# Odd blocks of the delta loop on the other partition half, inverse products on four 64x64 tiles

## The reference, cut to what matters

```python
def step(carry, ins):
    s, mem = carry
    qt, kt, vt, dt, at, bt = ins
    mem = DECAY * mem + dt
    ...                                   # spike of the membrane
    alpha = jax.nn.sigmoid(at + asp * spike)
    beta = jax.nn.sigmoid(bt[..., None] + jnp.sum(spike * bsp, -1, keepdims=True))
    ...
    s = s * alpha[..., None]
    pred = jnp.einsum('bhk,bhkv->bhv', kt, s)
    s = s + (beta * kt)[..., None] * (vt - pred)[:, :, None, :]
    out = jnp.einsum('bhk,bhkv->bhv', qt, s)
    return ((s, mem), out)
```

## Time and profile before

| | |
|---|---|
| median of three runs | 2595.97 us |
| profiled execution | 2596.74 us, span 2594.9 us |
| granted TensorE clock, mean | 0.862 of full speed |
| PE busy | 2186.4 us (84%), 32607 instructions |
| PEld busy | 1506.7 us (58%) |
| DVE busy | 1612.6 us (62%), 4155 instructions |
| ACT busy | 981.7 us (38%) |
| POOL busy | 781.0 us (30%) |
| L2317, ax | 5120 records, 193.9 us busy |
| L2339, xw | 4096 + 1024 records, 140.0 + 33.0 us busy |
| L2293, products of levels 0 to 5 | 6144 records, 128.7 us busy |
| L2308, the 2I of ax | 160 records, 65.1 us busy |

### The profile page before, as it was taken

How to read it: one execution, slowest core, us unless ns; L and a number is a source line. 1 busy time by engine, 2 the same in 40 slices (tenths; PEclk the granted TensorE clock), 3 DMA queues, 4 the chain that set the end, 5 groups by cost and what they waited for, 6 DMA issues and landing times. The chain is left out here.

```text
span 2594.9 us, 76890 instructions
## 1 busy us (share of the span) xinstructions
PE 2186.4 (84%) x32607; PEld 1506.7 (58%) x32607; DVE 1612.6 (62%) x4155; ACT 981.7 (38%) x1930; POOL 781.0 (30%) x884
## 2 busy tenths in 40 slices
PE   7999988999678658899999999999998968963774
PEld 4666656666556323656666666666666737652553
...
GB/s 168 10 10 2 10 10 6 2 2 2 78 37 68 77 118 18 3 27 3 23 7 23 7 23 7 23 7 2 7 3 7 3 54 48 2 33 15 52 53 125
DMA packets 42516, 75.98 MB, mean 29 GB/s; under 512 B 5988, under 2 KB 27244, under 8 KB 39620
## 3 DMA queue, kind: packets, MB, share of 16 engines
...
...
## 5 line engine op out<-in xcount | busy, mean ns | idle before, releaser
L2786 DVE COPY_PREDICATED delta_neg_a_and_p_t<-delta_level_int,bank 128x256 f32<-128x256 uint8 x384 | 179.5, 537 | 65.6 <-PE bank L2293 65.0
L2317 PEld LDWEIGHTS bank<-delta_inverse,delta_neg_a_and_p_t 64*64 64x64 f32 x5120 | 171.4, 141 | 46.1 <-issue 45.6
L2317 PE MATMUL bank<-delta_inverse,delta_neg_a_and_p_t 64*64 64x64 f32 x5120 | 193.9, 228 | 0.0
L2690 POOL TENSOR_TENSOR delta_scaled_beta_k<-delta_scaled_beta_k,delta_decays 128x256 f32<-128x256 f32 x160 | 124.2, 776 | 223.4 <-issue 165.2
L2520 ACT ACTIVATE delta_two_less_ax<-bank 128x512 f32<-128x512 f32 x160 | 94.9, 597 | 243.0 <-PE bank L2317 241.6
L310 PE MATMUL bank<-attn_w_value_out,attn_z_self_t 128*64 128x512 f32 x512 | 144.7, 680 | 40.4 <-DVE attn_cross_attended_t L722 36.3
L699 POOL TENSOR_TENSOR attn_probs<-attn_probs,attn_row_sum 128x512 f32<-128x512 f32 x64 | 65.4, 1042 | 359.4 <-DVE attn_row_sum L781 359.4
L2293 PE MATMUL bank<-weights_sb,delta_scaled_beta_k 64*64 64x64 f32 x6144 | 128.7, 229 | 46.5 <-DVE delta_neg_a_and_p_t L2786 40.8
L2293 PEld LDWEIGHTS bank<-weights_sb,delta_scaled_beta_k 64*64 64x64 f32 x6144 | 110.2, 141 | 82.8 <-DVE delta_neg_a_and_p_t L2786 48.7
L601 ACT ACTIVATE attn_probs_t<-bank 128x512 f32<-128x512 f32 x128 | 71.3, 595 | 197.8 <-PE bank L409 197.8
L2339 PE MATMUL bank<-delta_two_less_ax,delta_inverse_t 64*64 64x64 f32 x4096 | 140.0, 224 | 5.2 <-issue 5.2
...
...
## 6 DMA issues: line engine op xcount, KB each, us to landing
...
```

Of the source, the lines that this page charges most:

```text
L2317: last = pe.matmul(out_[rows(sg), u], AP[rows(sg), hp, eo, b4, 0, :], X[rows(sg), hp, u], start=False, stop=True, skip_group_check=True)
L2690: pool.tensor_tensor(r_[:, :, 0, :], r_[:, :, 0, :], a_[:, :, 1, 0:1].to_broadcast([128, T // (2 * c), c]), ALU.mult)
L2786: last = dve.copy_predicated(second(AP[:, hp, eo, :, :, :].rearrange("p b i n -> p (b i) n"), c), m_, PAIR[hp % 2][eo][:, :].rearrange("p ...
```

## The change

Nothing is computed differently; where things lie and on which part of the array they are multiplied changes, and so does the order.

- AP, X, XT and W have the parity of the block (eo) as their outermost dimension, and a head pair's even or odd units are 256 columns. For even blocks nothing moves. For odd blocks W, XT and the values now lie on the half r = par, where before they lay on sg; X and AP stay on sg. So in ax, xw and y the row half and the column half of odd blocks differ, and those of even blocks are equal.
- Work goes by pairs of head pairs, P = 0 or 1, two head pairs at a time. A product, an ax or an xw is 32 matmuls into two full banks (one for even, one for odd units), where it was 16 matmuls into two half-used banks (products) or one bank (inverse). The inverse has banks 4, 5 for P = 0 and 2, 3 for P = 1; the products of stages 3 to 6 of both P use banks 0 and 1.
- The 2I of ax is written by four bf16 matmuls of 64x64 by 512 columns for each P, where it was one of 128x128 by 512 for each head pair.
- DVE's masked copies take 512 columns where they took 256, half as many. An addition of first_inverse and a transpose of 128x512 becomes three instructions for each P: one of 128x512 for the even units, two of 64x512 for the odd ones, which write to the half that they don't read. Per group that is 30 transposes for 20 and 6 additions for 4. ACT's copies keep their size and number, except those of o (4 of 512 columns for 8 of 256).
- On PE ax(P=0) and ax(P=1) come first, then products and xw of P = 0, a filler, xw and products of P = 1. Norms are summed in two halves at different places, values in two halves ahead of and between the xw of the last level. On DVE a level is masked, scale, scale, turned for P = 0 and then the same for P = 1, where all four head pairs were masked and scaled before any was transposed.

```diff
-                AP = sb("neg_a_and_p_t", [128, HDP, 2, 4, 2, 64], ctx=ctx)
-                X = sb("inverse", [128, HDP, NU], ctx=ctx)
-                XT = sb("inverse_t", [128, HDP, NU], ctx=ctx)
-                W = sb("two_less_ax", [128, HDP, NU], ctx=ctx)
+                AP = sb("neg_a_and_p_t", [128, 2, HDP, 4, 2, 64], ctx=ctx)
+                X = sb("inverse", [128, 2, HDP, 256], ctx=ctx)
+                XT = sb("inverse_t", [128, 2, HDP, 256], ctx=ctx)
+                W = sb("two_less_ax", [128, 2, HDP, 256], ctx=ctx)
...
+                INV = ((bank[4], bank[5]), (bank[2], bank[3]))
+                OUT = ((bank[0], bank[1]), (bank[4], bank[5]))
+                STRAIGHT_AND_CROSSED = ((0, slice(0, 128), slice(0, 128)), (1, slice(0, 64), slice(64, 128)), (1, slice(64, 128), slice(0, 64)))
+
+                def hps(P):
+                    return slice(2 * P, 2 * P + 2)
+
+                def product_banks(stage_, P):
+                    return PAIR[P if stage_ < 3 else 0]
...
-                def units():
-                    for b in range(GB):
-                        for par in range(2):
-                            yield b, b % 2, b // 2, par, slice(64 * par, 64 * par + 64), par ^ (b % 2)
+                def units(P):
+                    for n in range(2):
+                        for b in range(GB):
+                            for par in range(2):
+                                yield (2 * P + n, b, b % 2, b // 2, par, slice(64 * par, 64 * par + 64), par ^ (b % 2),
+                                       slice(256 * n + 64 * (b // 2), 256 * n + 64 * (b // 2) + 64), n == 0 and b < 2)
...
-                            pe.matmul(out_[:, :], identb[:, :], eye2b[:, :].unsqueeze(1).to_broadcast([128, 8, 64]), start=True, stop=False,
-                                      skip_group_check=True)
...
-                                last = pe.matmul(out_[rows(sg), u], AP[rows(sg), hp, eo, b4, 0, :], X[rows(sg), hp, u], start=False,
-                                                 stop=True, skip_group_check=True)
...
+                        for eo in range(2):
+                            for sg in range(2):
+                                pe.matmul(INV[P][eo][rows(sg ^ eo), :], identb[rows(sg), rows(sg)],
+                                          eye2b[rows(sg), :].unsqueeze(1).to_broadcast([64, 8, 64]), start=True, stop=False,
+                                          skip_group_check=True)
+                        pe.wait_ge(s["masked"], 14 * g + 2 * (l + 1) + P + 1)
...
+                            last = pe.matmul(INV[P][eo][r, u], AP[rows(sg), eo, hp, b4, 0, :], X[rows(sg), eo, hp, b4 * 64:b4 * 64 + 64],
+                                             start=False, stop=True, skip_group_check=True)
+                        last.then_inc(s["w_ps"], 1)
...
-                                    lhsT, rhs = XT[rows(sg), hp, u], W[rows(sg), hp, u]
...
+                                last = pe.matmul(INV[P][eo][rows(sg), u], XT[r, eo, hp, n], W[r, eo, hp, n], start=first, stop=True,
+                                                 skip_group_check=True)
...
+                            last = pe.matmul(INV[P][eo][rows(sg), u], XT[r, eo, hp, b4 * 64:b4 * 64 + 64], Vt(g)[r, hp, 4 * eo + b4, :],
+                                             start=first, stop=True, skip_group_check=True)
...
+                            m_ = m_.unsqueeze(1).to_broadcast([128, 16, 32 // c, c])
                             for eo in range(2):
-                                last = dve.copy_predicated(second(AP[:, hp, eo, :, :, :].rearrange("p b i n -> p (b i) n"), c), m_,
-                                                           PAIR[hp % 2][eo][:, :].rearrange("p (u m c) -> p u m c", u=16, c=c)[:, 0:8, :, :])
+                                last = dve.copy_predicated(second(AP[:, eo, hps(P), :, :, :].rearrange("p h b i n -> p (h b i) n"), c), m_,
+                                                           two[eo][:, :].rearrange("p (u m c) -> p u m c", u=16, c=c))
...
-                    def turned(g, l, hp):
-                        dve.wait_ge(s["x"], 16 * g + HDP * (l - 1) + hp + 1)
-                        dve.transpose(XT[:, hp, :], X[:, hp, :]).then_inc(s["x_t"], 1)
...
+                    def turned(g, l, P):
+                        for eo, to, of in STRAIGHT_AND_CROSSED:
+                            dve.wait_ge(s["x"], 16 * g + 4 * (l - 1) + 2 * P + eo + 1)
+                            last = dve.transpose(XT[to, eo, hps(P), :].rearrange("p h n -> p (h n)"),
+                                                 X[of, eo, hps(P), :].rearrange("p h n -> p (h n)"))
+                        last.then_inc(s["x_t"], 1)
```

460 lines of the change are left out of this document (239 added, 221 removed).

## The result

The changed kernel takes 2620.36 us in the median (2599.01 to 2636.87, 20 runs) where the kernel before takes 2594.69 (2588.53 to 2600.32, 20 runs). The ratio is 1.0096, with 95% of its interval between 1.0079 and 1.0112: 26 us slower, where 83 us faster were forecast. The runs of the changed kernel spread over 38 us, those of the kernel before over 12, and the long ones have the lower clock: the run of 2599.01 us has a granted clock of 0.827, that of 2636.87 us 0.813. The profiled execution has a span of 2620.8 us, and the loop takes 1107.8 us of it, for 1080.4 before.

A forecast was written before the change was run, and what follows sets the result against it. PE was taken to set the pace, DVE close behind. After the change DVE's 120.0 us plus 12 us of waits make full groups 132 us; all groups together lose 83 us, giving 2513 us (range 2445 to 2570).

The forecast's parts named there:

- PE, part by part: PE's work per full group: xw 9.2, y 1.6 and ax 12 us less, in sum 22.8, so 132.4 becomes 109.6 us.
- the four bf16 matmuls: Writing 2I in ax on four different tiles: 0.5 us together, 0.31 if side by side, 1.24 if one after the other.
- The rule on row tiles and banks: Row tiles cannot access one PSUM bank at once; rival that the tiles bring nothing: 2597 to 2615 us, chance 0.07.
- DVE, part by part: DVE's occupied time per full group goes from 112.8 to 120.0 us, making it longer than PE by 10 us.
- Transposes: DVE, 30 for 20 per group at 0.60 us: 6.0 us more; crossed pieces, additions' included, 3.6 more (bounds 0 and 3.6).
- The additions: DVE's additions of the first inverse, 6 for 4 per group: 1.3 us more (1.3 to 1.7).
- The masked copies: DVE, 28 instructions of 512 columns for 56 of 256 per group: 1.7 us less (bounds 0 and 3).
- The membrane's operations: DVE, disturbed less by POOL's squares of q, which come earlier: 2 us less per group (bounds 0 and 3.7).
- Which waits stay ... Together 12 us (bounds 5 and 18): DVE's waits for PE in a full group: 12 us stay, which with 120.0 us occupied makes 132 us.
- a rival at 0.05 with 2619 us: PE's chain from last masked copies to next group's first product runs half at 1.2 GHz: 15 us more per group.
- My test, a granted clock under 0.9: Stated sign that the forecast is wrong: the granted clock of the loop falls under 0.9.
- PE goes on setting the pace: Rival, whole loop: DVE's waits shrink, each of 8 groups loses 22.8 us, giving 2414 us; chance 0.07.

The follow-up runs named there:

- e2: Changed kernel with two more products, their values overwritten, ahead of the wait for the first square at each group's start; ratio 0.9938 to before, full groups 141.4 us.
- e8: e2 with ScalarE crossing the odd blocks' half out of the bank and VectorE's pieces straight; 2560.97 us where the kernel before takes 2647.96, full groups 129.6 us.
- e6: e2 with six more products, their values overwritten, in TensorE's wait behind the membrane; ratio 0.9951 to before, full groups 142.3 us.
- e5: e2 with VectorE's additions and transposes straight and the crossing left out, so values are wrong; ratio 0.966 to before, full groups 129.7 us.
- e10: e8 with the gated product between VectorE's two first inverses and the fourth head-row product behind both output products; full groups 131.4 us.
- e7: e2 with the first 8 of 26 membrane steps moved into VectorE's wait at a group's start; ratio 0.9901 to before, full groups 140.7 us.
- e13: e8 with the four products of the sums of squares left out, so norms are wrong; ratio 0.9579 to before, full groups 128.4 us.
- e9: Changed kernel's order and wide copies, but inverse products on two tiles, VectorE's pieces straight, and e2's two products at a group's start; full groups 136.4 us.
- e12: e8 without the two more products at a group's start; 2549.60 us where the kernel before takes 2594.64.

## Why the prediction was wrong

**PE, part by part: right but for two stretches.** 64 records take 0.93 to 1.16 us; only the last level's xw still takes 2.08 us (1409.65), since there operands and result stand on the same half and two tiles do all. The description of the change has it with the others, and I had counted those two among the ten: 1.8 us too much. Then the four bf16 matmuls took 0.24 us (taken 0.5, bounds 0.31 and 1.24). The rule on row tiles and banks (the Trainium skill, TensorEngine Tiling (Array Packing), Gotcha 1: PSUM Pressure) did not hold here: 64 records that share two banks took 0.93 to 1.16 us. PE's busy time fell by 18 us in e2's seventh group (112 for 130 before) and by 17 in e8's full groups (115 for 132), with 2.1 us of added products in both. Without these that is 19 to 20 of the 22.8 us foretold; in e8 the clock was also lower (0.92 for 0.97 in the mean of the full groups), which hides some more.

**DVE, part by part: the sum was right, its terms were not.** The sum was 120.0 us occupied, the trace has 120.2. Transposes cost 8.3 us more per group for the 9.0 priced (6.0, and 3.0 of the 3.6), a triple being 2.17 us for the 2.1 priced. The pieces of a triple are 0.72 us apart and straight transposes 0.60. That fits the rule by which an instruction that starts in another quadrant than the one before it is held until all earlier ones are finished (the Trainium skill, VectorE: DVE Perf Modes, Two Vector instructions with no wait between them). The additions cost 3.8 us more, not 1.3: six of 1.07 and 1.28 us for four of 0.86, all beside work of GpSimd, as before. The masked copies gave back 2.6 us (foretold 1.7). The membrane's operations gave back 5.1 us and not 2.0. My 3.7 us "at most" counted 62 of its some 125 steps, and the others were stretched too. Against that the head-row gate (0.68 to 2.2 us), the normalised rows (0.28 to 0.61 us each) and the residual (0.73 to 1.3 us) lengthened by 3.5 us together. That the terms made 120.0 is luck in part.

**The step that failed: "Which waits stay ... Together 12 us (bounds 5 and 18)".** 29.6 us stayed. With the clock kept up it is 21.1 us (e2), and nearly the same (21.4 to 22.5) in the other kernels with four tiles, whether VectorE is occupied for 120 us (e6) or 108 (e5, e8, e10); only where VectorE's own steps were moved into a wait (e7, 17.0) or PE's work left out (e13, 19.1) it is less. Of e2's five full groups (busy us, mean ns of one | idle before, of which):

```profile
L2809 DVE COPY_PREDICATED delta_neg_a_and_p_t<-delta_level_int,bank 128x512 f32<-128x512 uint8 x120 | 101.5, 912 | 17.4 <-PE bank L2309 16.7
L2937 DVE SCALAR_TENSOR_TENSOR delta_scaled_beta_k<-weights_sb,bank 128x512 f32<-128x512 f32 x20 | 13.7, 687 | 25.6 <-PE bank L2204 25.4
L2926 DVE TENSOR_TENSOR weights_sb<-weights_sb,bank 128x512 f32<-128x512 f32 x20 | 13.7, 685 | 17.9 <-PE bank L2204 17.9
L2797 DVE COPY_PREDICATED delta_neg_a_and_p_t<-delta_level_int,bank 128x512 f32<-128x512 uint8 x20 | 13.4, 723 | 27.5 <-PE bank L2297 27.5
```

I had listed some waits that stay and let the rest go with PE's faster tiles. The wait for the feed-forward output did go (5.1 to 1.3 us). But a group waits 5.5 us for the first masked copies and 3.5 for the later ones, where I had 3.4 and 1.8, and 5.1 and 3.6 for scaled and beta-weighted keys (L2937, L2926), where I had 3.3 and a part of 2. The waits that grew or stayed are at the start and the end of a group. As I read it they are on chains over PE and ScalarE in which few instructions got faster; that is argued from the order and not shown, since e13 left it open. Before, the waits were 27.7 us in all, so the change took 6.6 us of them and I had credited it with nearly 16. That alone makes the full group 141.4 and not 132: the change would have brought nothing.

**The remaining 8.4 us are the clock**, which I had as a rival at 0.05 with 2619 us. That its time met the measured one is luck, since the mechanism was right only in half. I had put it on the chain from the last masked copies to the next group, 15 us per group, following the wait behind the membrane. That wait came (7.2 us) and the low clock behind it too, but it costs nothing (e6), and y, behind it, ran at full speed (1.16 us). The fall that costs is at the group's start, behind the wait that I had noted as growing since "no filler stands any more between o and the next group's first product", and had priced at its length alone. My test, a granted clock under 0.9, did fire. So did the wait of over 20 us, which I had tied to PE's pace and a time below 2450 us, where it stood for the opposite.

**In sum for a full group**: 140.3 before; the new order and the wide copies -3.9 (e9), the four tiles -6.8 (e8 against e9), the crossing on VectorE +11.8 (e2 against e8), the start's clock +8.4 (changed against e2): 149.8. These are steps along one row of kernels, so that they add up is no test; that the last two don't depend on one another is what e12 tested. The crossing, whose cost was in my sum for VectorE, takes away all that the tiles and the order give, and the clock then makes the loss. The rival that "PE goes on setting the pace" did not hold either: with PE at 132 us of 136 busy (e9) and at 115 of 130 (e8) the group differs by 6.8 us, not by 17. VectorE's path and its turnarounds set the pace: 12.1 us less of its occupied time (e8 against e2) gave 11.8 us.

The other groups missed too, by both their work and their waits: the first took 121.0 us (foretold 118.5; VectorE occupied for 110 as foretold, waits 11 for 8), the seventh 128.0 (117.5; PE busy 110.5 for 107 and without work 17.5 for 10.4), the last 109.7 (101; PE busy 86 for 82 and without work 24 for 19).
